# Masked cross-attention: one exponential of 2048 columns a head, three of four turned banks emptied by ScalarE, the diagonals formed by GpSimd

## The reference, cut to what matters

```python
def _L1_xattn_ref(q, k, v, mask, Wq, Wk, Wv, Wo):      # 16 heads of 32 columns
    qh = (q @ Wq.T).reshape(B, Sq, H, d).transpose(0, 2, 1, 3)
    kh = (k @ Wk.T).reshape(B, -1, H, d).transpose(0, 2, 1, 3)
    vh = (v @ Wv.T).reshape(B, -1, H, d).transpose(0, 2, 1, 3)
    scores = jnp.einsum('bhqd,bhkd->bhqk', qh, kh)
    scores = jnp.where(mask[:, None, :, :], jnp.float32(-1000000000.0), scores) * scale
    attn = jax.nn.softmax(scores, axis=-1)
    out = jnp.einsum('bhqk,bhkd->bhqd', attn, vh)
    return out.transpose(0, 2, 1, 3).reshape(B, Sq, Hd) @ Wo.T
...
x = x + _L1_xattn_ref(_layernorm(x), ctx, ctx, mask, ...)
x = x + _L1_attn_ref(_layernorm(x), ...)     # self-attention
x = x + _L1_ffn_ref(_layernorm(x), ...)      # eight experts, two for each row
```

## Time and profile before

| | |
|---|---|
| time, median of 3 runs | 1693.84 us (1692.97 to 1701.72) |
| the profiled execution's own time | 1694.49 us |
| its span | 1693.2 us |
| busy: PE, PEld, DVE, ACT, POOL | 1628.3, 1305.7, 1065.9, 908.3, 126.1 us |
| exponentials (L1374) | 256, 183.6 us |
| turned banks copied by ACT (L1382), by DVE (L1440) | 128 and 128, 75.0 and 88.1 us |
| diagonals on DVE (L1449) | 32, 13.6 us |

### The profile page before, as it was taken

One profiled execution on the slowest core, in us unless ns is written; L12 is line 12 of the kernel. 1 busy time (PEld: TensorE's weight loads), 2 busy tenths in 40 slices (PEclk: granted clock), 3 DMA queues, 4 the chain that ended last, 5 costly groups with the idle time before them and its releaser, 6 DMA issues.

```text
span 1693.2 us, 29865 instructions
## 1 busy us (share of the span) xinstructions
PE 1628.3 (96%) x11374; PEld 1305.7 (77%) x11374; DVE 1065.9 (63%) x2282; ACT 908.3 (54%) x1910; POOL 126.1 (7%) x75
## 2 busy tenths in 40 slices
PE   7999999998999999999999999999899988999998
PEld 5778888887878878989888888877555557777776
DVE  5777777685563424565656665699534437687865
ACT  6666766663144313545545554588323335676764
POOL 0000000000000002000100010000011102233223
PEclk9999999999999999999999999999999998999999
DMA  6332323222840269988868886789730044787852
GB/s 234 125 104 82 101 80 99 88 67 90 312 147 1 74 202 303 301 246 257 269 210 257 250 264 213 228 229 260 289 136 7 7 171 171 260 321 285 291 179 77
DMA packets 147260, 308.56 MB, mean 182 GB/s; under 512 B 11452, under 2 KB 101564, under 8 KB 135548
## 3 DMA queue, kind: packets, MB, share of 16 engines
q1 hardware_dynamic: 145564, 301.65, 55.1%
q0 software_dynamic: 1536, 4.76, 0.9%
HBM read 225.16 MB, written 81.22 MB: 181 GB/s over the span
## 4 chain that ended last, share of the span: by engine, by line
PE 84%; DVE 6%; ACT 4%; DMA 2%; issue 2%; DVEq 1%; SPq 0%; POOL 0%; ACTq 0%; POOLq 0%
PE bank L128 15%; PE bank L130 14%; PE bank L129 14%; PE bank L1306 6%; PE bank L1684 4%; PE bank L1328 3%; PE bank L2215 3%; PE bank L1296 3%; PE bank L2219 2%; PE bank L2216 2%; PE bank L2250 2%; PE bank L1783 2%; PE bank L1339 2%; ACT T L1834 1%; DVE WS L2532 1%
## 5 line engine op out<-in xcount | busy, mean ns | idle before, releaser
L1374 ACT ACTIVATE TT<-TT,MX 128x512 f32<-128x512 f32 x256 | 183.6, 722 | 2.5 <-DVE MX L1433 2.5
L2532 DVE TENSOR_TENSOR WS<-EW,WS 128x1024 fp32r<-128x1024 f32 (+1 forms) x120 | 147.9, 1243 | 57.3 <-ACT WS L2363 56.5
L1427 DVE CUSTOM_DVE_ANT_0 TT<-bank,MASK 128x512 f32<-128x512 f32 x256 | 174.1, 684 | 5.6 <-PE bank L1296 3.7
L2363 ACT CAST WS<-EW 128x1024 fp32r<-128x1024 f32 (+1 forms) x144 | 139.1, 977 | 50.9 <-PE bank L2219 49.5
L1306 PE MATMUL bank<-IDN,TT 128*128 128x128 f32 x1024 | 155.4, 275 | 4.6 <-DVE PT L1440 2.5
L128 PE MATMUL bank<-BCH,WKT 128*128 128x256 f32 x512 | 150.5, 294 | 3.7 <-DVE BCL L360 3.7
L1306 PEld LDWEIGHTS bank<-IDN,TT 128*128 128x128 f32 x1024 | 120.3, 140 | 36.9 <-issue 13.0
L130 PE MATMUL bank<-BCH,WKT 128*128 128x256 f32 x512 | 145.6, 284 | 0.0
L129 PE MATMUL bank<-BCL,WKT 128*128 128x256 f32 x512 | 145.5, 284 | 0.0
L335 ACT CAST EKH<-bank 128x512 fp32r<-128x512 f32 x64 | 37.4, 585 | 148.2 <-PE bank L130 138.7
L1440 DVE COPY PT<-bank 128x512 f32<-128x512 f32 x128 | 88.1, 688 | 43.6 <-PE bank L1306 43.6
(11 more groups left out here) (335 smaller groups left out, 3779.6 us busy)
## 6 DMA issues: line engine op xcount, KB each, us to landing
EW<-in_ewg SPq DMA_DIRECT2D x48, 1024.0 KB, 5.7
KST<-tmp_k SPq DMA_DIRECT2D x43, 768.0 KB, 6.2
tmp_k<-EKH SPq DMA_DIRECT2D x128, 256.0 KB, 3.3
EW<-in_ewg SPq DMA_DIRECT2D x24, 768.0 KB, 4.9
CT<-in_ctxT SPq DMA_DIRECT2D x32, 512.0 KB, 3.5
CN<-in_ctxN SPq DMA_DIRECT2D x32, 512.0 KB, 3.6
BCT<-in_ctxT SPq DMA_DIRECT2D x32, 512.0 KB, 4.5
tmp_k<-EKL SPq DMA_DIRECT2D x64, 256.0 KB, 3.1
```

Of the source, the lines that this page charges most:

```text
L1374: act.activation(TT[:, n % 4, cs], TT[:, n % 4, cs], ACT.Exp, bias=MX[:, n % 4, 5:6], scale=SC1, accum_out=SUM[:, b % 2, h, kc:kc + 1]).th ...
L1427: dve.tensor_tensor_reduce(TT[:, sl, 512 * kc:512 * kc + 512], bank[(0, 1, 4)[g % 3]][:], MASK[:, b % 2, 512 * kc:512 * kc + 512], 1.0, NE ...
L2363: act.copy(WS[:, i % NR, 0, 0:n * w], EW[q % NE][:, at:at + n * w]).then_inc(*w_high.up)
L2532: dve.tensor_tensor(WS[:, i % NR, 1, 0:n * w], EW[q % NE][:, at:at + n * w], f(WS[:, i % NR, 0, 0:n * w]), ALU.subtract).then_inc(*w_low.up)
```

## The change

Three edits, all in the cross-attention:

1. ACT makes one exponential of 2048 columns a head at the place where the first of the four stood, with one row sum; 64 instead of 256. PE's wait for it moves from one in every two steps to one in eight, for the whole head. SUM has one column a head.
2. ACT copies the turned banks of three of four steps (g % 4 is 0, 1 or 2), DVE only that of the fourth (g % 4 == 3): 192 and 64 copies instead of 128 and 128.
3. DVE's `pair_sums` keeps the reciprocal alone. The multiplication with the identity, and the wait for `sums_mm` of the pair before it, are GpSimd's, between its masks.

```diff
@@ -1254,11 +1254,11 @@
-        s_exp, p_act, o_kept = S.new("act", 256), S.new("act", 128), S.new("act", 32)
+        s_exp, p_act, o_kept = S.new("act", 64), S.new("act", 192), S.new("act", 32)
...
         def p_kept(g):
-            return (p_dve if g % 2 else p_act)[g // 2]
+            return p_dve[g // 4] if g % 4 == 3 else p_act[g - g // 4]
...
             def turn(g):                                   # cross_pe
                 p, pc, bk = g // 8, g % 8, turn_bank[g]
-                if pc % 2 == 0:
-                    pe.wait_ge(*s_exp[4 * (2 * p + 1) + pc // 2])
+                if pc == 0:
+                    pe.wait_ge(*s_exp[2 * p + 1])
...
-                b, h, cs = n // 16, n % 16, slice(512 * kc, 512 * kc + 512)
-                if kc == 0:
-                    act.wait_ge(*s_max[n])
-                act.activation(TT[:, n % 4, cs], TT[:, n % 4, cs], ACT.Exp, bias=MX[:, n % 4, 5:6], scale=SC1,
-                               accum_out=SUM[:, b % 2, h, kc:kc + 1]).then_inc(*s_exp.up)
+                if kc % 4 == 0:
+                    b, h, cs = n // 16, n % 16, slice(512 * kc, 512 * kc + 2048)
+                    if kc == 0:
+                        act.wait_ge(*s_max[n])
+                    act.activation(TT[:, n % 4, cs], TT[:, n % 4, cs], ACT.Exp, bias=MX[:, n % 4, 5:6], scale=SC1,
+                                   accum_out=SUM[:, b % 2, h, kc // 4:kc // 4 + 1]).then_inc(*s_exp.up)
 
             def turn(g):                                   # cross_act
-                if g % 2 == 0:
+                if g % 4 != 3:
...
             def turn(g):                                   # cross_dve
-                if g % 2:
+                if g % 4 == 3:
...
             def pair_sums(p):
                 b, c = p // 8, 2 * (p % 8)
-                dve.wait_ge(*s_exp[4 * (2 * p + 1) + 3])
-                own(dve.tensor_reduce(RS[:, c:c + 2], SUM[:, b % 2, c:c + 2, :], AX.X, ALU.add))
-                own(dve.reciprocal(RS[:, c:c + 2], RS[:, c:c + 2]))
-                if p:
-                    dve.wait_ge(*sums_mm[p - 1])
-                dve.tensor_tensor(DG, IDN[:].unsqueeze(1).broadcast_to([128, 2, 128]),
-                                  RS[:, c:c + 2].unsqueeze(2).broadcast_to([128, 2, 128]),
-                                  ALU.mult).then_inc(*sums_diag.up)
+                dve.wait_ge(*s_exp[1 * (2 * p + 1) + 0])
+                dve.reciprocal(RS[:, c:c + 2], SUM[:, b % 2, c:c + 2, 0]).then_inc(*sums_turned.up)
...
+            def pair_sums(p):                              # cross_pool
+                c = 2 * (p % 8)
+                pool.wait_ge(*sums_turned[p])
+                if p:
+                    pool.wait_ge(*sums_mm[p - 1])
+                pool.tensor_tensor(DG, IDN[:].unsqueeze(1).broadcast_to([128, 2, 128]),
+                                   RS[:, c:c + 2].unsqueeze(2).broadcast_to([128, 2, 128]),
+                                   ALU.mult).then_inc(*sums_diag.up)
+
             pool.wait_ge(*xq_mm[3])
-            for b in range(4):
-                load_mask(b)
+            load_mask(0)
+            load_mask(1)
+            for p in range(32):
+                pair_sums(p)
+                if p in (7, 15):
+                    load_mask(p // 8 + 2)
```

More of the change, by code:

```diff
@@ L1139, in build @@
         MX = A("MX", [128, 4, 8])
-        SUM = A("SUM", [128, 2, 16, 4])
+        SUM = A("SUM", [128, 2, 16, 1])
         RS = A("RS", [128, 16])
@@ L1256, in build @@
         sums_mm, wo_mm = S.new("pe", 32), S.new("pe", 32)
-        s_exp, p_act, o_kept = S.new("act", 256), S.new("act", 128), S.new("act", 32)
+        s_exp, p_act, o_kept = S.new("act", 64), S.new("act", 192), S.new("act", 32)
         cross_root = S.new("act", 3)
-        s_masked, s_max, p_dve = S.new("dve", 256), S.new("dve", 64), S.new("dve", 128)
-        sums_diag, o_scaled, x_added, cross_var = S.new("dve", 32), S.new("dve", 32), S.new("dve", 4), S.new("dve", 3)
-        mask_made = S.new("pool", 4)
+        s_masked, s_max, p_dve = S.new("dve", 256), S.new("dve", 64), S.new("dve", 64)
+        sums_turned, o_scaled, x_added, cross_var = S.new("dve", 32), S.new("dve", 32), S.new("dve", 4), S.new("dve", 3)
+        mask_made, sums_diag = S.new("pool", 4), S.new("pool", 32)
         ld_qs, ld_vg = ([S.keep("ld", 16) for _ in range(2)] for _ in range(2))
```

## The result

The changed kernel takes 1700.97 us in the median of 22 runs (1696.13 to 1711.85), the kernel before 1693.67 us in 22 runs beside it (1690.79 to 1704.41). The ratio is 1.0042, with a 95% interval of 1.0029 to 1.0055: 7.1 us slower (4.9 to 9.3). So the sign of the forecast was right and the size near: 1703 was predicted, for a distance of 8.6 us. The prediction called same what is within 0.5%; the result is on that side of the border, so of its two likely classes the one with the smaller chance came out (same 40%, slower 52%), and the interval reaches across the border.

What follows compares the result with a forecast made beforehand. PE was taken to bound up to 1088 us, then DVE and its handshake with PE. A loss of 10.9 less a credit of 2.3 gave +8.6 us on 1694.49, forecast 1703; range for 8 in 10: 1695 to 1712.

Steps and rivals of the forecast that it cites:

- What bounds: Cross-attention: PE full from 668 to 1088 us; then DVE and its handshake with PE set the pace for some ten pairs.
- the ring of banks: Pairs without background work: PE fills banks that ACT and DVE empty; both ways round close near 10.45 us, without slack.
- One exponential: ACT, each head: 2.00 us for 2048 columns instead of 2.86, from the casts' 0.837 ns a column; saves 0.86 us.
- Copies and diagonals: Each pair: ACT gains two copies, 1.0 us; DVE loses 1.2 us and the diagonal, which takes GpSimd 0.8 us, hidden.
- copy of step 5: ACT's 0.57 us copy of the bank step 7 needs; starts only after the odd head's 2.00 us exponential, ending at 5.95.
- The pair: Two heads without background work: 10.45 us a pair against 9.4 before.
- PE's standstill at step 7: Once a pair, PE stands still about 1.8 us before step 7, until ACT empties its bank.
- gross loss: Pairs without background work: 8.4 and 0.5 in nine, 0.4 in the first, 1.6 in one with few scores; together 10.9 us.
- The credit for the last keys: Near 1188 us: slower pairs shorten PE's 2.60 us wait for late keys and the low clock after it; 2.3 us gained.
- Relief wins: Pairs without background work: long exponentials meet empty banks, PE falls to its own 8.5 us a pair; 1689 us, 8%.
- Nothing moves: Whole kernel: the estimate misses slack, and loss and credit cancel; 1692 to 1698, say 1695 us, 10%.
- this rival: Pairs without background work: PE's 1.8 us standstills drop the clock to 1.2 GHz in every second pair; 1718 us, 10%.

Runs made afterwards that it cites:

- Version 3: Kernel before with only the diagonals moved to GpSimd, sum and reciprocal still on DVE: ratio to before 1.0005, 9.40 us a pair.
- 1: Kernel before with only one exponential of 2048 columns a head: ratio to before 1.0000, 9.66 us a pair.
- 2: Kernel before with only ACT copying three of four turned banks, exponentials of 512 columns: ratio to before 1.0004, 9.57 us a pair.
- 4: Changed kernel with each exponential split into two of 1024 columns: ratio to the kernel before 1.0000, 9.52 us a pair.
- 5: Changed kernel with DVE's two copies a pair at steps 1 and 5 instead of 3 and 7: ratio to the kernel before 1.0003, 9.66 us a pair.
- 12: Kernel before with the long exponential and ACT's three of four copies, diagonals still on DVE: ratio to before 1.0025, 10.38 us a pair.
- 9: Kernel before with the next stage's weight loads started at step 235 instead of 205: ratio to before 0.9989, 9.4 us a pair.
- version 10: Changed kernel with the next stage's weight loads started at step 235 instead of 205: ratio to the kernel before 1.0042, 10.38 us a pair.
- 11: Changed kernel with exponentials of 1024 columns, DVE copying at steps 1, 5 and 7, and weight loads later: ratio to the kernel before 0.9956, 9.34 us a pair.
- 8: Changed kernel with two exponentials of 1024 columns a head and DVE copying at steps 1, 5 and 7: ratio to the kernel before 0.9975, 9.35 us a pair.

## Why the prediction was right

- *What bounds.* PE full up to 1088 us, before and after: right. That DVE sets the pace behind it was only half right. Version 3 takes work and a wait off DVE and gains nothing, so it is rather the ring of banks, with DVE's copies in it, that sets the pace, and not DVE's 95%.
- *One exponential.* 2.01 us measured, 2.00 from the slope of the casts.
- *Copies and diagonals.* Diagonals at 0.62 us hidden: right. That neither edit costs much alone, and that exponential and copy of step 5 do so together, was the core of the argument, and the pairs of 1, 2, 4, 5 and 12 bear it out.
- *The pair.* 10.38 against 10.45. PE's standstill at step 7 is 1.57 us for the matmuls and 1.88 for the weight loads, against 1.8. Over the whole stretch the gross loss was given as 10.9 and is 10.2 (versions 9 and 10): 8.3 instead of 8.9 in the nine pairs, 0.4 as given in the first, 1.5 instead of 1.6 in the one with few scores.
- *The credit for the last keys* is the term that was mis-sized: 2.3 taken, from bounds of 1.05 and 5.6. The wait went wholly, 5.3 us with the clock behind it. But in the profile of the changed kernel the clock fell too, one pair later, behind a standstill of 1.81 us at 1204 us; that is the 1.6 which version 10 doesn't have. So the credit was 5.3 - 1.6 = 3.7 net, and 10.2 - 3.7 = 6.5 is what the profiles show (6.4). In the terms of the sum, one term was 3.0 too small and a loss of 1.6 was missing; that they partly cancel is luck. All of this is from one execution of each kernel, and the times don't confirm it (version 10). I had kept the credit low "because PE is still idle at the same place"; but the last keys, issued at 1184.33, were taken up at 1194.93 without a wait, 10.6 us later, where they had taken 12.5 before. The queue was less crowded: 223 GB/s from 1104 to 1180 us, before 246.
- *Rivals.* "Relief wins" is out (3, and the pair of the change). "Nothing moves" is out. The clock did not swing in the pairs: from 1104 to 1180 us it was 1.00 with a standstill of 1.6 us in each. It fell at the end, to 0.50 from 1206 to 1208 us, at a pair with few scores. So this rival came true once, and the sum had no term for it. The profiles of 12 and 5 show the same fall (batches of 2.48 and 2.42 us instead of 1.75 in that pair, behind standstills of 1.81 and 1.36). Version 10 has the same pair with the same standstill of 1.81 us at a clock of 1.00 throughout, so what decides it there stays open:

```profile
1202.00:1212.00 10.00, 7.95 (x102) 6.13 (x100) 1.75 (x4) 4.61 (x8) 0.61 (x1) 0.83 1.02 399
...
1206.00:1208.00 2.00, 2.00 (x32) 1.57 (x34) 0.00 (x0) 0.59 (x1) 0.53 (x1) 0.50 1.02 414
```
```profile
1195.00:1212.00 17.00, 14.22 (x222) 10.89 (x210) 4.90 (x13) 8.99 (x18) 0.61 (x1) 1.00 0.92 340
```

(The first two rows are of the changed kernel, the third of version 10.) The Trainium skill says in "TensorE: Matmul & The Clock Gate", section "A second HAM failure mode: psum-queue depth-cycling", that in a kernel which cycles through PSUM banks short idle times between groups of matmuls made the clock swing. The nine pairs here, with 1.57 us each at a clock of 1.00, do not agree.

## What to carry to other kernels

Count not only an engine's busy time but how long it is deaf, that is, how long it runs one instruction and can't start the next. A long instruction on an engine that also empties banks in a ring of two can be a wait of nearly its own length for whoever fills them (1.57 of 2.01 us here), unless the next bank to be emptied is another engine's. Fusing four instructions saved 0.86 us of ACT a head. Alone it cost 0.26 us a pair, with a copy of the other bank right behind it 0.98, and with the same load but the copies dealt out otherwise 0.26 again. And relief for the busiest engine was worth nothing in version 3, where the order of the hand-offs stayed.

## What I had not expected of the hardware

- Loads of 512 KB issued beside loads of keys of 768 KB delayed these. Starting the 18 loads of the next stage 35 steps earlier cost 14 us against the kernel before. Starting them 30 steps later gained nothing that is clear of noise: 1.9 us in 9, none in 10 against the changed kernel, 3.2 in 11 against 8. From 1050 to 1240 us the keys took 10.8 us in the median from issue to landing with the early weights, and 6.1 before:

```profile
KST<-tmp_k SPq DMA_DIRECT2D x15, 768.0 KB, 10.8
```
```profile
KST<-tmp_k SPq DMA_DIRECT2D x15, 768.0 KB, 6.1
```

- PE can stand still 1.6 us in every 10.4 and keep the full clock over those pairs. In the pair with few scores the clock fell behind 1.81 us in the changed kernel and in 12, and not in 10. The stage behind runs the same program in both kernels, and its mean clock was 0.97 in one profile and 0.95 in the other.
